# The causal mask of a decoder's first layer: sixteen 32 x 32 products in place of four full-array ones

## What is computed

```python
q, k, v = split(layernorm(x) @ w_qkv)              # 16 heads of 8 features
scores = einsum('bhcqd,bhckd->bhcqk', q, k) / HD ** 0.5
scores = where(causal, scores, -inf)               # key position <= query position
out = einsum(softmax(scores), v) @ w_out
```

## Time and profile before

| | |
|---|---|
| median of 3 runs | 462.06 us (461.74 to 462.36) |
| the profiled execution's own time | 461.92 us |
| its span, first to last instruction | 460.1 us |
| mean granted TensorE clock | 0.969 of full speed |
| PE busy | 419.9 us, 91% |
| DVE busy | 301.1 us, 65% |
| ACT busy | 165.5 us, 36% |
| POOL busy | 121.8 us, 26% |

### The profile page before, as it was taken

How to read it: one execution, slowest core, us unless ns; L and a number is a source line. 1 busy time by engine, 2 the same in 40 slices (tenths; PEclk the granted TensorE clock), 3 DMA queues, 4 the chain that set the end, 5 groups by cost and what they waited for, 6 DMA issues and landing times.

```text
span 460.1 us, 10649 instructions
## 1 busy us (share of the span) xinstructions
PE 419.9 (91%) x4083; PEld 275.4 (60%) x4083; DVE 301.1 (65%) x757; ACT 165.5 (36%) x475; POOL 121.8 (26%) x137
## 2 busy tenths in 40 slices
PE   2888999999999999999999999998497998959995
PEld 1345666677656566556655665566253543659994
DVE  4467758665675757765656665563667775955996
ACT  1134334343333433334334333433266882210000
POOL 1102212202221413132231432100863452330111
PEclk9889999999999999999999999999899999958999
DMA  7995000000000000000000000000000000000001
GB/s 240 315 282 129 5 1 1 2 1 1 2 1 2 2 1 1 5 2 1 1 1 2 2 1 1 1 2 1 1 1 1 1 0 2 2 0 1 25 24 46
DMA packets 12417, 12.85 MB, mean 28 GB/s; under 512 B 2360, under 2 KB 9416, under 8 KB 12112
## 3 DMA queue, kind: packets, MB, share of 16 engines
q1 hardware_dynamic: 12368, 12.18, 9.0%
HBM read 11.13 MB, written 1.05 MB: 26 GB/s over the span
## 4 chain that ended last, share of the span: by engine, by line
PE 81%; DVE 8%; ACT 4%; issue 4%; POOL 1%; DMA 1%; SPq 0%; POOLq 0%; DVEq 0%; ACTq 0%
PE ps L936 12%; PE ps L848 8%; PE ps L881 7%; PE ps L845 7%; PE ps L878 7%; PE ps L1103 6%; PE ps L895 6%; PE ps L856 4%; PE ps L923 3%; PE ps L1001 2%; PE ps L947 2%; PE ps L1093 2%; PE ps L1049 2%; PE ps L911 2%; ACT p_sb L757 2%
## 5 line engine op out<-in xcount | busy, mean ns | idle before, releaser
L672 ACT ACTIVATE pT<-ps 128x512 f32<-128x512 f32 x128 | 66.1, 602 | 90.5 <-PE ps L856 90.5
L563 POOL TENSOR_TENSOR rstd<-veps,minus_half 128x1 f32<-128x1 f32 x32 | 19.0, 593 | 188.1 <-DVE veps L287 188.1
L325 DVE TENSOR_REDUCE m_pad<-ps 128x8 f32<-128x1024 f32 x32 | 39.1, 1221 | 23.0 <-PE ps L881 22.8
L298 DVE TENSOR_TENSOR p_sb<-qk_sb,heads 128x512 f32<-128x512 f32 x48 | 45.4, 948 | 1.1 <-ACT qk_sb L686 1.1
L895 PEld LDWEIGHTS ps<-pT,p_sb 128*32 128x32 f32 x1024 | 26.0, 109 | 23.7 <-ACT pT L672 23.6
L334 DVE RECIPROCAL rden<-ps 128x16 f32<-128x16 f32 x32 | 8.2, 258 | 47.7 <-PE ps L816 47.7
L328 DVE TENSOR_REDUCE m_pad<-ps 128x8 f32<-128x1024 f32 x32 | 38.8, 1213 | 0.0
L881 PE MATMUL ps<-p_sb,qk_sb 32*128 32x512 f32 x256 | 37.2, 652 | 0.0
L347 DVE TENSOR_TENSOR x_sb<-x_sb,ps 128x128 f32<-128x128 f32 x32 | 9.2, 288 | 41.4 <-PE ps L923 41.4
L895 PE MATMUL ps<-pT,p_sb 128*32 128x128 f32 x1024 | 34.6, 276 | 0.7 <-ACT pT L672 0.7
L572 POOL TENSOR_TENSOR cm<-onehot,ctx_sb 128x1024 f32<-128x1024 bf16 x16 | 34.3, 2144 | 1.3 <-DVE onehot L355 1.3
(11 more groups left out here) (156 smaller groups left out, 818.4 us busy)
## 6 DMA issues: line engine op xcount, KB each, us to landing
itok_i<-itok SPq DMA_DIRECT2D x1, 1024.0 KB, 7.5
wkv_sb<-wkv SPq DMA_DIRECT2D x1, 1024.0 KB, 12.6
tk<-fside SPq DMA_DIRECT2D x1, 1024.0 KB, 8.1
out<-itok_i SPq DMA_DIRECT2D x8, 128.0 KB, 1.8
x_sb<-x SPq DMA_DIRECT2D x1, 768.0 KB, 5.2
x_sb<-x SPq DMA_DIRECT2D x1, 256.0 KB, 2.9
pad_words<-pad SPq DMA_DIRECT2D x1, 256.0 KB, 6.9
w_qkv_sb<-w_qkv SPq DMA_DIRECT2D x1, 192.0 KB, 2.9
```

Of the source, the lines that this page charges most:

```text
L298: return dve.tensor_tensor(dst, rows.unsqueeze(1).broadcast_to([128, QUADS, S]), heads[:, 0, :].unsqueeze(2).broadcast_to([128, QUADS, S]) ...
L325: dve.tensor_reduce(m4[:, 0:2, 0:QUADS], ps[:, 0:2, :].rearrange("p g (j k) -> p g j k", j=QUADS), AX.X, ALU.max).then_inc(s["max_low"], 1)
L672: act.activation(pT[:, t % 2, g, :, :], quad[4 + g], ACT.Exp).then_inc(s["exped"], 1)
```

## The change

The mask of turns 0 to 15 is put into the four banks by sixteen products of 32 rows and 32 columns of the array, 512 columns each: row group g works for bank g, column group c makes its partitions 32c to 32c + 31. The stationary operand is a 32 x 32 identity, `ident_bf[group(g), group(g)]`, and the moving operand is row group g's own copy of the mask's rows 32c to 32c + 31. So `causal` has a further dimension of four and is loaded with 2 KB per partition in place of 512 bytes. In `scores_by_query` the four waits now stand before the sixteen products of a turn below 16. The masks of turns from 16 on are made as before.

```diff
-        causal = sb("causal", [128, 2, 128], bf16)
+        causal = sb("causal", [128, 2, QUADS, 128], bf16)
...
+            def causal_tiles(first, side):
+
+                for c in range(QUADS):
+                    for g in range(QUADS):
+                        pe.matmul(quad[first + g][32 * c:32 * c + 32], ident_bf[group(g), group(g)],
+                                  causal[group(g), side, c, :].unsqueeze(1).broadcast_to([32, QUADS, S]),
+                                  start=True, stop=False, skip_group_check=True)
+
...
-                mask = causal[:, 1, :] if t < B else xmaskT[:, t - B, :]
-                for g in range(QUADS):
-                    pe.matmul(quad[4 + g], ident_bf[:, :], mask.unsqueeze(1).broadcast_to([128, QUADS, S]),
-                              start=True, stop=False, skip_group_check=True)
+                if t < B:
+                    causal_tiles(4, 1)
+                else:
+                    for g in range(QUADS):
+                        pe.matmul(quad[4 + g], ident_bf[:, :],
+                                  xmaskT[:, t - B, :].unsqueeze(1).broadcast_to([128, QUADS, S]),
+                                  start=True, stop=False, skip_group_check=True)
...
-                mask = causal[:, 0, :] if t < B else xmask[:, t - B, :]
                 for g in (0, 1, 3, 2):
                     if g == 0 and t >= 1:
                         pe.wait_ge(s["mT_copied"], t)
...
-                    pe.matmul(quad[g], ident_bf[:, :], mask.unsqueeze(1).broadcast_to([128, QUADS, S]),
-                              start=True, stop=False, skip_group_check=True)
+                    if t >= B:
+                        pe.matmul(quad[g], ident_bf[:, :],
+                                  xmask[:, t - B, :].unsqueeze(1).broadcast_to([128, QUADS, S]),
+                                  start=True, stop=False, skip_group_check=True)
+                if t < B:
+                    causal_tiles(0, 0)
```

More of the change, by code:

```diff
@@ L214, in _ @@
             sp.dma_start(heads[:, :, :], c_heads).then_inc(s["consts_in"], 16)
-            sp.dma_start(causal[:, :, :], c_causal).then_inc(s["consts_in"], 16)
+            sp.dma_start(causal[:, :, :, :], c_causal).then_inc(s["consts_in"], 16)
             sp.dma_start(ident_bf[:, :], c_ident_bf).then_inc(s["consts_in"], 16)
@@ L1150 @@
                               -(p[:, None] % 32 == _np.arange(QUADS)).astype(_np.float32)], axis=1),
-        "c_causal": _np.stack([_np.where(p[:, None] >= p, 0.0, -MASKED), _np.where(p[:, None] <= p, 0.0, -MASKED)],
-                              axis=1).astype(bf),
+        "c_causal": _np.stack([_np.stack([_np.where(flip * (32 * c + p[:, None] % 32 - p) >= 0, 0.0, -MASKED)
+                                          for c in range(4)], axis=1) for flip in (1, -1)], axis=1).astype(bf),
         "c_samepos": _np.where(p[:, None] % 8 == p[None, :] % 8, 0.0, MASKED).astype(bf),
```

## The result

The changed kernel takes 447.42 us (median of 4 runs, 446.36 to 447.99), the kernel before 461.90 us on the same chip (4 runs, 461.57 to 462.36): a ratio of 0.9683, 95% interval 0.9662 to 0.9705, or 14.5 us less. The forecast was 450.6, the range 446.5 to 457.5. One execution among all those reported here, of the last experiment, fell in a slow state (514.10 us at a mean granted clock of 0.75, where the other three took 440.64 to 441.01 at 0.97) and is left out of that experiment's median.

The account below looks back on a forecast made before the run. PE was taken to bound the first layer's steady part, unless another engine's chain comes up. Savings of 9.1 + 2.8 - 0.4 = 11.5 us off the median 462.06 gave 450.6 us, range 446.5 to 457.5.

Parts of the forecast that it names:

- The products: Mask blocks at L878 and L845: sixteen tiles starting 0.01 us apart, new block 0.46 us, saving 0.51 and 0.49.
- The three rivals on this step: Mask blocks: half rate in array, 453.5 to 454.5; issue sets pace, 457.5; column strips in turn, 464; chance 0.10 each.
- the last one's worse case with bare loads: Column strips of one row strip in turn, loads bare in three later rounds: 0.33 us more per block, up to 474.
- The change of shape: Key side, L845 after the full-array transposes: changing tile shape adds 0.03 us, bounds 0 and 0.09; L845 saves 0.46.
- The waits: scores_by_query, bank waits now before all sixteen products: cost taken as 0; 1.2 us if 0.1 each time over 12 turns.
- Where PE stops being the limit: Periods 2 to 15: savings arrive only where DVE is not level; 0.97 us per full period at most, 9.1 in sum.
- The 0.2 us for restarts: After periods 7, 9 and 13 PE waits at L800 and loses loads made ahead: 0.07 us each, -0.2 us.
- The start: Before the first L800: the half-clock L878 block saves 0.9 us, the larger mask load costs 0.4.
- The load: causal growing from 64 to 256 KB delays ident_bf and DVE's first work: 0.4 us, bounds 0 and 0.8.
- The block of period -1: L878 at half clock takes 1.89 us; the new block near 0.9, so 0.9 saved.
- The clock: Periods 0 and 1 each hold a half-clock stretch costing the same whatever work lies in it; 0.97 us saved each.
- Later stretches: One half-clock stretch more or less, at the start or in the last third: 1.4 us either way.

Follow-up runs that it names:

- the last experiment: Changed kernel with POOL's L572 held back until DVE's first maximum, and heads given its own semaphore: 440.79 us (median of three), ratio 0.9556.
- L572 edit: Changed kernel with POOL's large product (L572) held back until DVE has taken the period's first maximum: 441.51 us, ratio 0.9563 against the kernel before.

## Why the prediction was right, and where its sizes were off

*The products.* The mechanism was right: row and column strips together, sixteen at once. The size was taken too large. I put 0.01 us from start to start, and the sixteen are there in a window closing 0.05 us after the first, so about 3.4 ns each; with the 0.31 after the last start the block is 0.36. That is 0.10 less per block than forecast, and it is most of the difference between 8.2 and 9.4 us in periods 3 to 15. The three rivals on this step fell in one run (each block twice), and so did the last one's worse case with bare loads.

*The change of shape.* 0.03 was taken at the key side; L829 starts 0.20 us after L823 (95.10 to 95.30) where L845 started 0.17 after it: 0.03. In periods that follow a wait at L800 it is up to 0.34, which belongs to the restart below.

*The waits.* 0 was taken. L829 starts 0.60 after L867's first in period 9 (97.15 to 97.75), as L878 did after L856 (108.48 to 109.08), and so it is in every period from 3 to 14, so the four waits in front cost nothing.

*Where PE stops being the limit.* Right period by period (table above), 3, 5 and 11 with nothing, 7 and 9 with 0.85, 13 with 0.57. It rested on one choice, that DVE's second L298 ends where POOL's L572 lets it, whatever its start. The L572 edit shows it: without the overlap L298 takes 0.69, and all seven periods give way. In all nine periods from 3 to 14 in which the two meet, that L298 ends 0.55 us after L572, before and after the change. The 0.2 us for restarts was too small: periods 8, 10 and 14, which follow such a wait in 7, 9 and 13, are 10.10, 10.04 and 9.53, where they are 9.88, 9.88 and 9.43 without it (the L572 edit), 0.48 us together. All of it lies between L800 and the first mask product, where the transposes come 0.85 us in place of 0.64 before L829 in period 8.

*The start.* The load was put at 0.4, with bounds 0 and 0.8. By L263 it is 0.5 in the first pair of profiles and 1.0 in the second. The block of period -1 was to take 0.9 and to save 0.9: it takes 0.58 at half clock (12.19 to 12.77), where it took 1.82 (11.68 to 13.50), so it saves 1.2. Behind it the clock rose 0.5 us later than before (at 15.5 for 15.0 us), and the first L800 came 0.52 earlier, for 0.5 in the forecast. That this fits so well is luck: the block gave more than forecast, the load and the later rise took it back, and in the second pair L800 came only 0.23 earlier (17.80 and 17.57).

*The clock.* The forecast took it that both half-clock stretches stay, and in the profiled execution of the changed kernel they were gone. 0.97 us each were counted for periods 0 and 1, and they gave 5.08 together. 3.25 of that is two half-clock stretches which this profile of before had and the second one of the same kernel hasn't. Against the second profile of before (7.43 and 7.53) the gain is 1.11 and 0.72, 1.83 in all, near the 1.94 of the forecast; period 1 gives less than two blocks, because DVE's one-hots end it, which I had overlooked. So of the 14.5 us between the medians some part may be where such stretches fell, and not the change; for the executions without a profile this is not shown. The single executions of before went from 459.5 to 462.4 us, those of the changed kernel from 446.4 to 448.6. With no stretch in the first 35 us on either side the two took 459.51 and 446.36, 13.2 us apart (one execution each, not taken together). By terms: 0.5 at the start, 1.8 in periods 0 and 1, 1.05 and 9.4 in 2 to 15 make 12.8. So of the 3 us by which the change brought more than the 11.5 forecast, 1.3 are the shorter blocks (periods 2 to 15); the rest stays open, and stretches of the clock are of that size.

*Later stretches.* The clock also falls near 312 and 387 us, as near 330 and 404 before. Period 16 to the end takes 285.7 and 286.0 us in the two profiles of the changed kernel, 285.2 and 286.3 in those of before; I had put 1.4 either way.

## What to carry to other kernels

Where the same small stationary matrix is put into several PSUM banks, sixteen tiles of 32 x 32, each row group with its own bank and its own copy of the moving rows, stream in the time of one product in place of four (a block of 0.36 us in place of 0.95 to 0.97); splitting the columns alone takes as long as before. Before counting the gain, set the next engine's chain beside the shortened one in each period, with the work on a third engine that holds it up: here an elementwise product on DVE ended 0.55 us after POOL's, whatever its start, and moving POOL's product was worth another 5.3 us. And profile the kernel before twice: a single profile had 3.25 us in it that another execution of the same program has not.

## What was not expected of the hardware

- Products on different 32 x 32 tiles start 3.4 ns apart, loads included (sixteen within a window of 0.05 us); on 32 x 128 tiles it was within 0.01. In these windows of the changed kernel, which close at 97.77 and 97.80, seven and then sixteen products have begun:

```profile
97.75 0.41 PE L829 MATMUL ps<-causal,ident_bf 32*32 32x512 bf16 x7
...
97.75 0.43 PE L829 MATMUL ps<-causal,ident_bf 32*32 32x512 bf16 x16
```

- A weight load costs nothing even when it goes to the tile whose own product is still streaming: sixteen such loads and products added 0.22 to 0.23 us, what one product streams.
- Four PSUM banks take the results of sixteen bf16 tiles at once with no loss of pace (0.22 us for 512 columns on sixteen tiles, as for 512 columns on the full array).
- A DVE product of two SBUF operands (L298, 0.66 us alone) that meets a POOL product of the same kind (L572, 2.14 us) ended 0.55 us after it in both kernels. It took 1.85 us when it started 0.84 after L572 and 2.42 when it started 0.28 after.
- TensorE's clock in the first 35 us differs between executions of one program: two falls to half clock, of 3.4 us each, or none (kernel before); a first rise at 15.5 or at 21.2 us (changed kernel). A fall or the late rise costs 1.6 us.
